# Weighing the values for two key blocks at a time in the second layer's attention, with sixteen places of exponentials

## The chip, the cores and the metric

The program runs on one core of a Trainium2 chip (NeuronCore 0 of one chip; the other cores are idle). The metric is the device time of one execution in microseconds, median of several runs. The program holds four layers; the change touches the attention of the second one (called layer 1 in the code, since counting starts at 0).

## The reference

Four layers, each `x = x + s * silu(ffn(xn))` with `s` an attention of the normalised input. The second layer's attention is a plain softmax attention over all keys (no causal mask), with 16 heads of 8 numbers each, 8 sequences of 512 tokens, after which only the 153 "most peaked" queries of a head keep their result:

```python
xn = _layernorm(x, axis=-1)
s = _L1_attn_ref(xn, Wq, bq, Wk, bk, Wv, bv, Wo, bo)    # scores, softmax, values; no mask
g = _silu(_L1_ffn_ref(xn, router_w, ...))                # routing to 64 small experts
x = x + s * g
```

For one head the part that matters here is: scores = q k^T (512 x 512), E = exp(scale * scores - maximum of the row), result = E^T v and the row sums of E, which come from a column of ones that is appended to v (hence 9 columns of values, 8 + 1).

## The kernel before, in words

`attend_phase` does this for both the first layer (causal) and the second (not causal, `maps = 1`). In the second layer the 128 pairs of sequence and head are worked on four at a time: 32 groups, called g below, of four heads each (UN = 4). The 512 tokens are four blocks of 128 (QT = 4). All engines run the same loop over groups, each in its own written order, and meet at semaphores.

For every group there are these steps:

- **First pass** (`pass1`, L686, TensorE): scores with queries in the rows, in 8 cells of two matrices 128 x 512 each, into `att_pS`, which has two places (SB = 2) for such a cell. VectorE takes the maximum of each row (`extreme`, L834, 128 x 1024 per cell) and frees the place. The first pass of group g + 2 is done while the exponentials of group g run.
- **Turning the maxima** (`turn_maxima`, L697, TensorE, waits for all 8 maxima of the group), and `negate` (L785, ScalarE); GpSimd then splits the maxima into three bf16 parts (L598, L601), and three DMAs (L569) put them beside the queries, as extra rows of the second product.
- **Second pass** (`pass2`, L708, TensorE): scores with keys in the rows, 16 cells c = 0..15 of 128 x 512 (cell c is key block c // 4 of head c % 4), into `att_pX`, which has three places (XB = 3). So `pass2` of cell c waits until the exponential of cell c - 3 is out of its place.
- **Exponentials** (`expo`, L779, ScalarE): one 128 x 512 instruction for each cell, from `att_pX` into `att_E`, which has NE places.
- **Weighing the values** (`weigh`, L721, TensorE): for one key block kt, four fp32 products of 9 x 512, one for each head, side by side in different columns of the array; each shows as two matmuls, so a call shows as x8. It waits until the exponentials of cells 4 kt to 4 kt + 3 are there. The four key blocks add up in `att_pO`.
- **Results**: ScalarE copies `att_pO` (`results`, L791, for the previous group), TensorE turns the copy (`turn_results`, L729), VectorE takes reciprocals and multiplies (`store`, L848, L851). Routing of the same layer's experts is done beside it on GpSimd and VectorE (L1546 to L1633).

The order of the work on TensorE is set by a loop over s = 0..15 for each group. In step s it first issues what PLAN[s] holds (a cell of the first pass at every even s; at s = 2 `turn_maxima` goes ahead of it, at s = 8 `turn_results`), then `pass2` of cell s + 1, and then whatever `WEIGHS` has under s. A key of 16 or more in `WEIGHS` means step s - 16 of the next group. On ScalarE, `expo` of cell s comes at step s, `negate` behind s = 1 and `results` behind s = RESULTS. Semaphores hold counts, so an engine can run ahead only as far as the places of `att_pX`, `att_pS` and `att_E` go.

Of the kernel before, what the change touches and what calls it, by code (L numbers as in the profile page):

```python
# [465 lines left out]
def attend_phase(nc, R, name, maps, arr, vtok, heads, lamb=None, negmax=None, aside=None):  # L466
# [13 lines left out]
    if causal:  # L480
        CELLS = [((0, 1, 2, 3), 0), ((0, 1), 1), ((0,), 2), ((2, 3), 1), ((1,), 2), ((0,), 3), ((2,), 2), ((3,), 2), ((1,), 3), ((2,), 3), ((3,), 3)]
        PLAN = ((0, 1),) + tuple((c,) for c in range(2, 11))
        XCELLS = [((x, 0),) for x in range(UN)] + [((x, 1), (x, 3)) for x in range(UN)] + [((x, 2), (x + 1, 2)) for x in range(0, UN, 2)]
        ORDER = (0, 1, 3, 2)
        WEIGHS = {7: (0,), 12: (1, 3, 2)}
        SEQ = (0, 1, "tops", 2, 3, 4, 5, 6, "turned", 7, 8, 9, 10)
        RESULTS, STORES = 3, {0: (0,), 1: (1,)}
        SB, XB = 4, 3
        NE = len(XCELLS)
    else:  # L490
        CELLS = [((x, x), j) for x in range(UN) for j in range(0, QT, 2)]
        PLAN = tuple((s // 2,) if s % 2 == 0 else () for s in range(16))
        XCELLS = [((x, kt),) for kt in range(QT) for x in range(UN)]
        ORDER = (0, 1, 2, 3)
        WEIGHS = {4: (0,), 8: (1,), 12: (2,), 16: (3,)}
        SEQ = (0, "tops", 1, 2, 3, "turned", 4, 5, 6, 7)
        RESULTS, STORES = 2, {0: (0, 1)}
        SB, XB = 2, 3
        NE = 8
    NP1, NP2 = len(CELLS), len(XCELLS)  # L500
    cell_of = {xk: c for c, cell in enumerate(XCELLS) for xk in cell}
    ready = {kt: 1 + max(c for (x, k), c in cell_of.items() if k == kt) for kt in range(QT)}
# [14 lines left out]
    with phase(nc, name) as p:  # L517
# [4 lines left out]
        mp = p.sb("mp", [IT, 2, 3, P], BF16)  # L522
        E = p.sb("E", [P, NE, T])
        vs = p.sb("vs", [P, 2, GH, QT, DV])
# [31 lines left out]
        with nc.Block() as block:  # L556
# [98 lines left out]
            def _(pe):  # L655
# [43 lines left out]
                def pass2(at, g, c, early):  # L699
                    k = (g * NP2 + c) % (NB * NP2)  # L700
                    bank, free = BANK2[k], g * NP2 + c + LAST2[k] + 1
                    if c == 0:
                        pe.wait_ge(s_mr[g % NB], at(48, 48 * (g // NB + 1)))
                    if not (early and free <= 0):
                        pe.wait_ge(s_e, at(NB * NP2, free))
                    for n, (x, kt) in enumerate(XCELLS[c]):
                        o, w = offset[x, kt], T - q0(kt)
                        ins = nc.tensor.matmul(pX[:, bank, o:o + w], ks[:, g % NB, x, kt * P:(kt + 1) * P], qs[:, g % NB, x, q0(kt):],  # L708
                                               start=(n == 0), stop=True, skip_group_check=True)
                    ins.then_inc(s_p2, 1)  # L710

                def weigh(at, g, kt, early):
                    if kt == 0:
                        pe.wait_ge(s_vs, of(at, 1, g, 1))
                        if not early:
                            pe.wait_ge(s_oT, of(at, 1, g, 0))
                    pe.wait_ge(s_cut if causal else s_e, of(at, NP2, g, ready[kt]))
                    w = T - q0(kt)
                    for x in range(UN):
                        o = offset[x, kt]  # L720
                        ins = nc.tensor.matmul(pO[32 * x:32 * x + DV, q0(kt):], vs[:, g % 2, x // maps, kt], E[:, cell_of[x, kt] % NE, o:o + w],  # L721
                                               start=(kt == ORDER[0]), stop=(kt == ORDER[-1]), tile_position=(0, 32 * x), skip_group_check=True)
                    ins.then_inc(s_pv, 1)
# [8 lines left out]
                def body(i, first, last):  # L732
# [9 lines left out]
                    for g in range(NB):  # L742
                        for s in range(NP2):
# [8 lines left out]
                            if not (last and h >= NB):  # L752
                                pass2(at, h, (s + 1) % NP2, first and h == 0)
                            for kt in WEIGHS.get(s + NP2, ()):
                                if not (first and g == 0):
                                    weigh(at, g - 1, kt, first and g == 1)
                            for kt in WEIGHS.get(s, ()):
                                weigh(at, g, kt, first and g == 0)
                    if last:
                        for s in range(NP2, 2 * NP2):  # L760
                            for kt in WEIGHS.get(s, ()):
                                weigh(at, NB - 1, kt, False)
# [5 lines left out]
            def _(act):  # L768
                def expo(at, g, c, first):
# [3 lines left out]
                    act.wait_ge(s_p2, of(at, NP2, g, c + 1))  # L773
                    if x == 0 and not (first and g == 0 and c < NE):
                        old = c - NE
                        held = max(ORDER.index(k) for _, k in XCELLS[old % NP2])
                        act.wait_ge(s_pv, of(at, QT, g, old // NP2 * QT + held + 1))
                    gain_of = x // maps
                    nc.scalar.activation(E[:, c % NE], pX[:, BANK2[(g * NP2 + c) % (NB * NP2)]], ACT.Exp, scale=gs[:, g % 2, gain_of:gain_of + 1]).then_inc(s_e, 1)  # L779

# [257 lines left out]
def layer0_attention(nc, R, t, early, out):  # L1038
    with ExitStack() as ctx:
        keep = lambda name, shape: ctx.enter_context(nc.sbuf_tensor(name, shape, F32))  # L1040
        heads = keep("heads0", [P, B * NH * QT, DH])
        vtok = keep("v0", [P, B * NH, QT, DH + 1])
        parts = nc.dram_tensor("parts0", (2, B * NH, 2, 3, DH, T), BF16).ap()
        with phase(nc, "arr0") as p:
            arr = Arrivals(p, 2, parts, R.ext0, t["gain0"], R.masks, t["later0"])
            project_phase(nc, R, "proj0", 4, early, parts, vtok, arr, qscale=True)
            attend_phase(nc, R, "att0", 2, arr, vtok, heads, lamb=R.lam)
        outproj_phase(nc, R, "out0", heads, out)
# [441 lines left out]
def layer1_attention(nc, R, t, early, out, sc, consts, s_in, comb, cT):  # L1490
    with ExitStack() as ctx:
        keep = lambda name, shape: ctx.enter_context(nc.sbuf_tensor(name, shape, F32))
        heads = keep("heads1", [P, B * NH * QT, DH])
        vtok = keep("v1", [P, B * NH, QT, DH + 1])
        negmax = keep("negmax", [P, B * NH * QT])
        total = keep("total", [P, B * QT, NH])
        mask = keep("mask1", [P, QT, B * NH])
        parts = nc.dram_tensor("parts1", (2, B * NH, 1, 3, DH, T), BF16).ap()
        with phase(nc, "arr1") as p:
            arr = Arrivals(p, 1, parts, R.ext1, t["gain1"])  # L1500
            project_phase(nc, R, "proj1", 2, early, parts, vtok, arr, mean={"sum": total})
            with routing(nc, "route", sc, consts, s_in, comb) as aside:
                attend_phase(nc, R, "att1", 1, arr, vtok, heads, negmax=negmax, aside=aside)
        with phase(nc, "spread") as p:
            pick_phase(nc, R, "pick", negmax, total, int(0.6 * 256), mask, comb, 64, cT, p.sem("out"))
        outproj_phase(nc, R, "out1", heads, out, mask=mask)
# [2170 lines left out]
```

## Time and profile before

| | us |
|---|---|
| median of 3 runs | 3879.37 (3876.12 to 3881.76) |
| the profiled execution | 3873.31 |
| its span, first to last instruction | 3871.5 |
| second layer's attention loop, first to last exponential | 1253.5 to 1674.5 |

In the span TensorE's matmuls are busy 87%, VectorE 61%, ScalarE 52%, GpSimd 40%. These shares are averages over stages with different limits; for this change only the stretch of the attention loop of the second layer matters. There `turn_maxima` (L697) comes once in every group, which makes it a good mark: it starts at 1272.22 us, and 29 groups later at 1653.2 us, which is 13.14 us for a group. Busy times of TensorE contain the drain of a matmul that overlaps the next one, so they are read for starts rather than for shares.

### The profile page before, as it was taken

Reading aid. Unit: us, or ns where it says so; the run is one execution under the profiler, and the core shown is the slowest. Engines: PE = TensorE matmul, PEld = TensorE weight load, DVE = VectorE, ACT = ScalarE, POOL = GpSimd, SP = SyncE. Lnnn points to the kernel's source line nnn. Section 1 sums busy time; section 2 is a strip of 40 time slices with the busy share of each in tenths; the row PEclk is TensorE's granted clock in tenths of the full one; section 3 lists DMA queues with packets and bytes.
Section 4 is the critical chain, followed back from the end, with each engine's and each line's share of the span. In section 5 each row is a group of like instructions: output and inputs, shape, how many; then the busy total and the mean of one; then the engine's idle time right before and its main releaser. Section 6 shows DMA issues by size and latency. Waiting matters only on the chain. (4 is left out here: it accounts for less than half of the span.)

```text
span 3871.5 us, 87522 instructions
## 1 busy us (share of the span) xinstructions
PE 3381.1 (87%) x26932; PEld 2090.2 (54%) x26932; DVE 2358.0 (61%) x5961; ACT 2030.5 (52%) x4194; POOL 1567.7 (40%) x2652
## 2 busy tenths in 40 slices
PE   5799999599966999959999947979874999999997
PEld 2344444477742222226777723579863666666664
DVE  5688887311135888856777765258356566666664
ACT  5588888333353788833333353333253566666552
POOL 0367676000010232316777717045472444444440
PEclk9799999799986999979999968877696999999999
DMA  5422222000013111116666411300023333333330
GB/s 138 102 73 74 73 73 54 12 6 12 6 36 89 45 44 46 41 27 173 163 156 161 117 58 37 102 12 3 9 50 55 127 115 114 118 115 113 114 101 22
DMA packets 199845, 289.31 MB, mean 75 GB/s; under 512 B 40954, under 2 KB 156864, under 8 KB 199252
## 3 DMA queue, kind: packets, MB, share of 16 engines
q1 hardware_dynamic: 195480, 277.41, 25.8%
q0 software_dynamic: 4096, 8.40, 1.5%
q8 instruction: 158, 2.59, 0.3%
q14 instruction: 111, 0.91, 0.1%
HBM read 234.41 MB, written 35.93 MB: 70 GB/s over the span
## 5 line engine op out<-in xcount | busy, mean ns | idle before, releaser
L779 ACT ACTIVATE att_E<-att_pX,att_gs 128x512 f32<-128x512 f32 x1152 | 718.7, 684 | 128.3 <-PE att_pX L708 127.6
L1958 POOL TENSOR_TENSOR att_E<-att_E,att_rz 128x128 f32<-128x128 f32 (+3 forms) x512 | 358.2, 721 | 433.6 <-DVE att_rz L2166 433.6
L834 DVE TENSOR_REDUCE att_mx<-att_pS 128x2 f32<-128x1024 f32 (+2 forms) x448 | 434.6, 991 | 82.2 <-PE att_pS L686 68.3
L686 PE MATMUL att_pS<-arr_ks,arr_qs 72*128 72x512 bf16 (+4 forms) x1536 | 421.4, 338 | 51.8 <-DVE att_mx L834 28.4
L708 PE MATMUL att_pX<-arr_qs,arr_ks 75*128 75x512 bf16 (+4 forms) x1536 | 419.2, 328 | 8.5 <-DMA arr_qs<-att_mp 4.4
L1698 POOL TENSOR_TENSOR pairs_h<-pairs_m,pairs_r 128x512 f32<-128x512 f32 x272 | 346.1, 1273 | 190.9 <-DVE pairs_m L1761 181.7
L1722 PEld LDWEIGHTS pairs_po<-pairs_a,pairs_h 128*128 128x128 f32 x2176 | 286.3, 192 | 130.3 <-issue 128.5
L826 DVE CUSTOM_DVE_ANT_0 att_seen<-att_pS,arr_later 128x384 bf16<-128x384 f32 (+1 forms) x512 | 298.8, 613 | 80.3 <-PE att_pS L686 79.9
L1743 ACT ACTIVATE pairs_r<-pairs_ph 128x512 f32<-128x512 f32 x272 | 162.6, 598 | 327.1 <-PE pairs_ph L1714 327.1
L721 PE MATMUL att_pO<-att_E,att_vs 128*9 128x512 f32 (+3 forms) x3072 | 296.8, 488 | 8.8 <-ACT att_E L779 8.4
L2097 ACT ACTIVATE att_E<-att_S,att_nm 128x128 f32<-128x128 f32 (+3 forms) x512 | 282.1, 556 | 39.6 <-DVE att_nm L2160 39.4
L1714 PE MATMUL pairs_ph<-xnT,pairs_a 128*128 128x512 f32 x544 | 281.4, 600 | 10.2 <-DMA pairs_a<-in_down_dram 10.2
L1722 PE MATMUL pairs_po<-pairs_a,pairs_h 128*128 128x128 f32 x2176 | 287.5, 275 | 0.3 <-POOL pairs_h L1698 0.3
L617 POOL TENSOR_SCALAR_AFFINE_SELECT att_E<-att_E 128x256 f32<-128x256 f32 (+1 forms) x640 | 228.5, 361 | 136.4 <-ACT att_E L779 131.1
L686 PEld LDWEIGHTS att_pS<-arr_ks,arr_qs 76*128 76x128 bf16 (+1 forms) x1536 | 133.9, 98 | 258.9 <-DVE att_mx L834 100.0
L1761 DVE SCALAR_TENSOR_TENSOR pairs_m<-pairs_ph,pairs_c 128x512 f32<-128x512 f32 x272 | 187.9, 692 | 140.4 <-ACT pairs_r L1743 132.2
L2160 DVE CUSTOM_DVE_ANT_0 att_S<-att_pS,att_bias 128x128 f32<-128x128 f32 (+3 forms) x512 | 230.5, 487 | 67.4 <-PE att_pS L2000 62.0
L708 PEld LDWEIGHTS att_pX<-arr_qs,arr_ks 127*128 127x128 bf16 (+1 forms) x1536 | 149.0, 98 | 217.0 <-ACT att_E L779 124.4
L1340 PEld LDWEIGHTS ex_po<-ex_a,ex_h 128*128 128x128 f32 x1536 | 201.6, 192 | 91.8 <-issue 91.0
L1366 ACT ACTIVATE ex_h<-ex_ph,ex_bs 128x512 f32<-128x512 f32 x192 | 132.0, 687 | 213.5 <-PE ex_ph L1331 213.5
L1382 DVE SCALAR_TENSOR_TENSOR f<-ex_po,ex_ws,f 128x128 f32<-128x128 f32 x192 | 54.1, 344 | 276.7 <-PE ex_po L1340 276.7
L2174 DVE COPY att_WT<-att_pT 128x128 f32<-128x128 f32 (+2 forms) x384 | 178.8, 507 | 66.2 <-PE att_pT L2010 59.0
(410 smaller groups left out, 6531.1 us busy)
## 6 DMA issues: line engine op xcount, KB each, us to landing
pairs_c<-weights SPq DMA_DIRECT2D x272, 256.0 KB, 4.0
att_bias<-in_bias_dram SPq DMA_DIRECT2D x64, 896.0 KB, 4.6
parts<-proj_part SPq DMA_DIRECT2D x144, 128.0 KB, 2.3
att_xb<-xnT SPq DMA_DIRECT2D x64, 256.0 KB, 2.7
arr_qs<-parts SPq DMA_DIRECT2D x192, 64.0 KB
arr_ks<-parts SPq DMA_DIRECT2D x192, 64.0 KB
att_w<-in_w3a_dram SPq DMA_DIRECT2D x64, 192.0 KB, 2.4
arr_qs<-parts SPq DMA_DIRECT2D x96, 96.0 KB
```

The lines of the kernel that those rows point to most:

```text
L686: ins = nc.tensor.matmul(pS[:, bank, n * w:(n + 1) * w], qs[:K1, u, x, q * P:(q + 1) * P], ks[:K1, u, x, :w], start=(n == 0 or not causal) ...
L708: ins = nc.tensor.matmul(pX[:, bank, o:o + w], ks[:, g % NB, x, kt * P:(kt + 1) * P], qs[:, g % NB, x, q0(kt):], start=(n == 0), stop=True ...
L721: ins = nc.tensor.matmul(pO[32 * x:32 * x + DV, q0(kt):], vs[:, g % 2, x // maps, kt], E[:, cell_of[x, kt] % NE, o:o + w], start=(kt == OR ...
L779: nc.scalar.activation(E[:, c % NE], pX[:, BANK2[(g * NP2 + c) % (NB * NP2)]], ACT.Exp, scale=gs[:, g % 2, gain_of:gain_of + 1]).then_inc( ...
L826: V.tensor_tensor_reduce(out=seen[:, own, :w], in0=pS[:, bank, :w], in1=arr.later[:, T - w:], scale=1.0, scalar=-3.0e38, op0=ALU.add, op1= ...
L834: V.reduce_max(dst, src, AX.X).then_inc(s_mx, 1)
L1698: nc.gpsimd.tensor_tensor(h[:, g % RING], m[:, g % RING], r[:, g % RING], ALU.mult).then_inc(s_h, 1)
L1714: nc.tensor.matmul(ph[:, g % RING], a[:, v, 0], R.xnT[:, b * T:(b + 1) * T], start=True, stop=True).then_inc(s_up, 1)
L1722: ins = nc.tensor.matmul(po[:, g % RING, q * P:(q + 1) * P], h[:, g % RING, q * P:(q + 1) * P], a[:, v, 1], start=True, stop=True)
L1958: nc.gpsimd.tensor_tensor(E[:, k, :width(j)], E[:, k, :width(j)], rz[:, u, k:k + 1].broadcast_to([P, width(j)]), ALU.mult).then_inc(s_n, 1)
L2097: nc.scalar.activation(E[:, k, :width(j)], S[:, r % RING, :width(j)], ACT.Exp, bias=nm[:, u, k:k + 1], scale=-1.0, accum_out=Z[:, u, k:k + ...
L2160: nc.vector.tensor_tensor_reduce(out=S[:, r % RING, :w_], in0=pS[:, r // 2 % 2, h, :w_], in1=bias[:, u, off:off + w_], scale=-1.0 / DW, sc ...
```

## The change

Four numbers in the branch for attention without a mask.

```diff
-        WEIGHS = {4: (0,), 8: (1,), 12: (2,), 16: (3,)}
+        WEIGHS = {9: (0, 1), 17: (2, 3)}
         SEQ = (0, "tops", 1, 2, 3, "turned", 4, 5, 6, 7)
-        RESULTS, STORES = 2, {0: (0, 1)}
+        RESULTS, STORES = 3, {0: (0, 1)}
         SB, XB = 2, 3
-        NE = 8
+        NE = 16
```

Key blocks 0 and 1 are weighed together at step 9, key blocks 2 and 3 together at step 1 of the next group. `att_E` gets 16 places instead of 8, since eight exponentials must now be kept until they are weighed. The copy of the results goes behind the exponential of cell 3 instead of cell 2. The instructions are the same in number and kind; the first layer's branch is not touched.

On TensorE, in the written-out first groups of the second layer's attention, around the step from one group to the next (`att_pX` is the second pass, `att_pS` the first pass, `att_pO` the weighing, `ident,att_mx` the turning of the maxima), there stood before:

```order
L721 MATMUL att_pO<-att_E,att_vs 9x512 x4
L708 MATMUL att_pX<-arr_qs,arr_ks 128x512
L686 MATMUL att_pS<-arr_ks,arr_qs 128x512 x2
L708 MATMUL att_pX<-arr_qs,arr_ks 128x512 x2
L686 MATMUL att_pS<-arr_ks,arr_qs 128x512 x2
L708 MATMUL att_pX<-arr_qs,arr_ks 128x512
L721 MATMUL att_pO<-att_E,att_vs 9x512 x4
L708 MATMUL att_pX<-arr_qs,arr_ks 128x512
L697 MATMUL att_pS<-ident,att_mx 16x128
L686 MATMUL att_pS<-arr_ks,arr_qs 128x512 x2
L708 MATMUL att_pX<-arr_qs,arr_ks 128x512 x2
```

And now at the same place:

```order
L721 MATMUL att_pO<-att_E,att_vs 9x512 x8
L686 MATMUL att_pS<-arr_ks,arr_qs 128x512 x2
L708 MATMUL att_pX<-arr_qs,arr_ks 128x512 x2
L686 MATMUL att_pS<-arr_ks,arr_qs 128x512 x2
L708 MATMUL att_pX<-arr_qs,arr_ks 128x512 x2
L686 MATMUL att_pS<-arr_ks,arr_qs 128x512 x2
L708 MATMUL att_pX<-arr_qs,arr_ks 128x512 x2
L686 MATMUL att_pS<-arr_ks,arr_qs 128x512 x2
L708 MATMUL att_pX<-arr_qs,arr_ks 128x512 x2
L721 MATMUL att_pO<-att_E,att_vs 9x512 x8
L697 MATMUL att_pS<-ident,att_mx 16x128
```

The weighing of two key blocks stands as one piece directly in front of the turning of the maxima, and a second-pass cell that stood between weighing and turning now stands ahead of the weighing. The other pair, the first row of the second piece, is followed by a first-pass cell and only then by second-pass cells; before, a second-pass cell always came first behind a weighing.

On ScalarE, in the same groups (`att_m<-att_pS` is `negate`, `att_oT<-att_pO` is `results`), before:

```order
L785 ACTIVATE att_m<-att_pS 16x128
L779 ACTIVATE att_E<-att_pX,att_gs 128x512
L791 ACTIVATE att_oT<-att_pO 128x512
L779 ACTIVATE att_E<-att_pX,att_gs 128x512 x15
L785 ACTIVATE att_m<-att_pS 16x128
```

And now:

```order
L785 ACTIVATE att_m<-att_pS 16x128
L779 ACTIVATE att_E<-att_pX,att_gs 128x512 x2
L791 ACTIVATE att_oT<-att_pO 128x512
L779 ACTIVATE att_E<-att_pX,att_gs 128x512 x14
L785 ACTIVATE att_m<-att_pS 16x128
```

Only the copy of the results has moved, by one exponential. VectorE, GpSimd and the DMA queue of SyncE have the same rows as before.

## Rows read from the trace of the kernel before

**Rows 1.** Stretches of the attention loop; busy us (instructions) by engine, clock, DMA

```profile
core 0: us, PE busy (x) PEld busy (x) DVE busy (x) ACT busy (x) POOL busy (x), PEclk, DMA share, GB/s
1256.00:1300.00 44.00, 40.66 (x210) 11.50 (x208) 34.28 (x59) 33.53 (x57) 10.88 (x31) 0.92 0.20 42
1300.00:1640.00 340.00, 317.35 (x1791) 95.60 (x1789) 285.23 (x458) 275.50 (x466) 102.65 (x293) 1.00 0.18 45
```

**Rows 2.** ScalarE's groups of instructions over 29 groups, 1272.2 to 1653.2

```profile
L779 ACT ACTIVATE att_E<-att_pX,att_gs 128x512 f32<-128x512 f32 x464 | 292.1, 681 | 57.9 <-PE att_pX L708 57.9
L791 ACT ACTIVATE att_oT<-att_pO 128x512 f32<-128x512 f32 x29 | 16.5, 570 | 0.0
L785 ACT ACTIVATE att_m<-att_pS 16x128 f32<-16x128 f32 x29 | 7.7, 267 | 14.5 <-PE att_pS L697 14.5
```

**Rows 3.** VectorE's and the weight loads' groups over the same 29 groups

```profile
L834 DVE TENSOR_REDUCE att_mx<-att_pS 128x2 f32<-128x1024 f32 x232 | 279.5, 1220 | 56.7 <-PE att_pS L686 55.0
L1613 DVE TENSOR_TENSOR route_eq<-route_gs 128x256 f32<-128x256 f32 x8 | 3.3, 412 | 0.0
...
L721 PEld LDWEIGHTS att_pO<-att_E,att_vs 128*9 128x9 f32 x928 | 14.0, 88 | 54.2 <-ACT att_E L779 37.0 <-issue 17.2
```

**Rows 4.** Timeline of one group, selected rows; idle before and releaser in brackets

```profile
1456.04 0.28 PE L697 MATMUL att_pS<-ident,att_mx 128*16 128x128 f32 x1
1456.35 0.27 ACT L785 ACTIVATE att_m<-att_pS 16x128 f32<-16x128 f32 x1 [0.43 <-PE att_pS L697]
1456.53 0.66 ACT L779 ACTIVATE att_E<-att_pX,att_gs 128x512 f32<-128x512 f32 x1
...
1457.10 0.57 ACT L791 ACTIVATE att_oT<-att_pO 128x512 f32<-128x512 f32 x1
1457.61 1.84 ACT L779 ACTIVATE att_E<-att_pX,att_gs 128x512 f32<-128x512 f32 x3
...
1458.37 1.05 PE L721 MATMUL att_pO<-att_E,att_vs 128*9 128x512 f32 x8
...
1459.04 1.78 SPq L569 DMA_DIRECT2D arr_qs<-att_mp  x3
...
1459.35 0.39 PE L708 MATMUL att_pX<-arr_qs,arr_ks 75*128 75x512 bf16 x1
...
1459.77 1.92 ACT L779 ACTIVATE att_E<-att_pX,att_gs 128x512 f32<-128x512 f32 x3 [0.32 <-PE att_pX L708]
...
1460.44 0.60 PE L729 MATMUL att_pS<-ident,att_oT 128*128 128x128 f32 x4
...
1461.49 0.60 PE L686 MATMUL att_pS<-arr_ks,arr_qs 72*128 72x512 bf16 x2 [0.45 <-DVE att_mx L834]
...
1462.35 0.69 ACT L779 ACTIVATE att_E<-att_pX,att_gs 128x512 f32<-128x512 f32 x1 [0.66 <-PE att_pX L708]
...
1463.65 2.50 ACT L779 ACTIVATE att_E<-att_pX,att_gs 128x512 f32<-128x512 f32 x4 [0.61 <-PE att_pX L708]
...
1464.08 2.36 DVE L834 TENSOR_REDUCE att_mx<-att_pS 128x2 f32<-128x1024 f32 x2 [0.72 <-PE att_pS L686]
...
1466.46 2.51 ACT L779 ACTIVATE att_E<-att_pX,att_gs 128x512 f32<-128x512 f32 x4 [0.32 <-PE att_pX L708]
...
1469.69 0.27 ACT L785 ACTIVATE att_m<-att_pS 16x128 f32<-16x128 f32 x1 [0.72 <-PE att_pS L697]
```

**Rows 5.** Timeline in the first layer: weighing of three key blocks in one piece

```profile
507.11 1.48 PE L721 MATMUL att_pO<-att_E,att_vs 128*9 128x384 f32 x24
508.53 0.34 PE L686 MATMUL att_pS<-arr_ks,arr_qs 76*128 76x384 bf16 x1
```

**Rows 6.** Timeline of the loop's first group and its end, and what follows the end

```profile
1260.02 1.90 PE L721 MATMUL att_pO<-att_E,att_vs 128*9 128x512 f32 x8
...
1675.23 1.04 PE L721 MATMUL att_pO<-att_E,att_vs 128*9 128x512 f32 x8 [1.14 <-ACT att_E L779]
1677.00 0.66 PE L729 MATMUL att_pS<-ident,att_oT 128*128 128x128 f32 x4 [0.72 <-ACT att_oT L791]
```

## The prediction

> **What bounds the kernel now.** I read the stretches of the attention loop first [rows 1]. From 1300 to 1640 us VectorE is busy 285.23 of 340 us (84%), ScalarE 275.50 (81%), GpSimd 102.65, and the granted clock is 1.00 throughout. No engine is full; TensorE's 317 us hold overlapped drains and say little. So the loop is held by engines that wait for each other, and what counts is who waits. The groups of ScalarE over 29 groups of heads [rows 2] say it: in 381.0 us, 13.14 a group, ScalarE sat idle 57.9 us for second-pass cells and 14.5 us for the turned maxima, together 2.50 us a group, and for nothing else. It never waited for a place in `att_E` or for `att_pO`. VectorE sat idle 55.0 us for first-pass cells [rows 3]. Both wait for TensorE, which works its list in order. The timeline of one group [rows 4] shows what stood in front each time. ScalarE's gaps are:
>
> - 0.43 (0.72 in the next group, 0.50 in the mean) ahead of `negate`: `turn_maxima` stands behind the weighing of block 3.
> - 0.32 ahead of exponential 6, and 0.32 ahead of 14: the second-pass cell stands behind the weighing of blocks 0 and 2.
> - 0.66 and 0.61 ahead of 9 and 10: TensorE turns the results, waits 0.45 for VectorE with first-pass cell 4, then weighs block 1.
>
> They sum to 2.34 with the 0.43, and to 2.63 with the 0.72 that the next group shows.
>
> **Durations**, all from rows 4. Exponentials follow each other by (2.50 - 0.69) / 3 = 0.60 us, `negate` takes 1456.53 - 1456.35 = 0.18 of ScalarE's line, `results` 0.51. A 128 x 512 bf16 product takes 0.60 - 0.39 = 0.21 of TensorE's line and is there 0.39 after its start; ScalarE starts 0.03 later. Weighing starts at 1458.37, and the next product at 1459.35: 0.98. A turned maximum is there after 0.28. Exponential 3 started at 1457.61 and frees ScalarE at 1458.21, and the weighing that needs it starts 0.16 later; I use 0.18 from "ScalarE could go on" to "TensorE may start". VectorE's maxima follow each other by 2.36 - 1.22 = 1.14 (1.22 is the mean of rows 3).
>
> These reproduce two gaps of before. Behind the weighing of block 0: 0.18 + 0.98 + 0.39 + 0.03 = 1.58, and ScalarE has two cells in hand (1.21): gap 0.37, the row says 0.32. Ahead of `negate`: 0.18 + 0.98 + 0.21 (a second-pass cell) + 0.31 = 1.68, less 1.21: 0.47, the rows say 0.43 to 0.72.
>
> **Weighing two blocks in one piece** is not in this loop, but the first layer weighs three blocks in one piece, 384 + 128 + 256 = 768 columns, in 508.53 - 507.11 = 1.42 us [rows 5]. Against 0.98 for 512 columns that is 0.44 / 256 = 1.72 ns a column, so 1024 columns take 0.98 + 0.88 = 1.86. The bounds are 1.96 (two single pieces) and 1.76 (1.72 ns each, no start at all). I take 1.86, as rows 5 are the same form. So TensorE saves 0.10 for each pair, 0.20 a group.
>
> **The change, part by part.** Sixteen places of `att_E`: worth nothing by themselves, since no wait for a place shows [rows 2]. Moving `results` by one exponential: nothing, it waits for nothing now and would still be late enough (below). What costs is the length of the piece against the three places of `att_pX`: when TensorE is away for 1.86 us, ScalarE has at most 3 x 0.60 = 1.81 in hand, and the second-pass cell isn't the first thing behind the piece any more.
>
> I walk a group from the moment 0 at which ScalarE is through with exponential 15.
>
> *Ahead of `negate`.* TensorE gets cell 15's place at 0.18, does second-pass cell 2 (to 0.39), weighs blocks 2 and 3 (to 2.25), turns the maxima; `negate` can start at 2.25 + 0.31 = 2.56. ScalarE ran out at 1.21. Gap 1.35, where it was 0.50.
>
> *Up to exponential 8.* `negate` 0.18, exponentials 2 and 3, `results` 0.51 (block 3 was weighed by 2.3, so no wait), exponentials 4 to 7: ScalarE is at 2.56 + 0.18 + 0.51 + 6 x 0.604 = 6.87. No weighing stands in steps 2 to 8, so the gaps ahead of 6, 9 and 10 are gone. VectorE gets first-pass cell 1 at 2.47 + 0.63 = 3.10 and does cells 1, 2, 3 by 6.52. First-pass cell 4 waits for the place of cell 3 as before, starts at about 6.64 and ends at 7.07; second-pass cells 9 and 10 follow, and cell 9 is just in time for ScalarE (7.49 against 7.47).
>
> *Ahead of exponential 11.* Weighing starts at 7.50, ends at 9.36; first-pass cell 5 takes 0.43; second-pass cell 11 is read at 9.79 + 0.42 = 10.21. ScalarE did 8, 9 and 10 by 8.68. Gap 1.53. If VectorE hadn't held TensorE up, it would be 0.18 + 0.21 + 1.86 + 0.43 + 0.42 - 1.81 = 1.29. Exponentials 11 to 15 then run through.
>
> So the gaps are 1.35 + 1.53 = 2.88 a group against 2.50. One group in four VectorE also has two routing comparisons of 0.41 [rows 3], which come just behind cell 4 in the order; I add 0.07 a group. My walk makes the gaps of before about 0.05 too long in one place of two (0.37 for 0.32), so I take off 0.05: +0.40 a group. The chain for the next group's maxima (GpSimd, then the DMAs issued at 1459.04) starts 0.85 later against ScalarE's line; its rows must be there for cell 0 of the next group some 9 us after the issue, and land long before [rows 4].
>
> *Sum.* 31 groups x 0.40 = 12.4 us. At the end of the loop, behind the last exponential, two blocks are weighed instead of one: +0.88. At its start the clock is at its lower level (1.2 GHz: 1.90 for a weighing instead of 1.05 [rows 6], mean clock 0.92 over 44 us [rows 1]), and a weighing of that time now comes after the rise: about -0.9. The two cancel. Profiled execution: 3873.3 + 12.4 = 3885.7 us. The median of the runs is 6.1 above the profiled execution, so I expect **3891.5 us** for it, +0.3%.
>
> **Bounds of this case.** With 1.76 for the pair and VectorE never late, 0.44 less a group: 0 us. With 1.96 and 0.2 more for routing: +0.8 a group, 25 us. So 3880 to 3904.
>
> **Rivals.**
>
> 1. *Faster: TensorE's order is the bound, and the joined piece takes waits out of it.* For it: weight loads of the weighing sat idle 37.0 us for an exponential [rows 3], 1.28 a group, four waits. In the new order the piece stands behind a second-pass cell that waits for the same exponential, so the piece has no wait of its own. If half of them go and the 0.20 is saved too, 0.84 x 31 = 26 us: 3853. Against it: TensorE waited there because it was ahead; ScalarE's gaps come from what follows. It decides if ScalarE's two new gaps stay under 1.2 each. Chance 0.12. The Trainium skill (Perfetto Trace Analysis, Matmul Optimizations) advises matmuls back to back in batches because of the clock, which speaks for this rival; the row shows a granted clock of 1.00 already, so by the rule there is nothing for the clock to give, and no number above rests on it.
> 2. *The same: VectorE decides.* It is busiest (84%), and with two first-pass cells in hand (2.28) it can ride over a piece of 1.86. If the round goes by VectorE, ScalarE's gaps only join into fewer and longer ones: 3879. Against it: VectorE's own idle time, 56.7 us for 29 groups, is waiting for TensorE, and my walk gives it a new wait of over 1 us behind the first piece. Chance 0.17.
> 3. *Slower by more: the clock.* At the lower level a weighing costs 0.85 more [rows 6]. If longer pauses of TensorE let the clock fall in one group of four, 8 groups with two pairs at +1.7 add 27 us: 3918. In the loop the clock never fell though waits of 0.4 to 0.9 us are all over it. Chance 0.03.
>
> The forecast itself has 0.68. A measurement of this kernel tells a change from none at about 0.2%, 8 us. Within the forecast's case about one in ten lies under that. Slower by over 0.2%: 0.63; within: 0.22 (rival 2 and the low end); faster: 0.15 (rival 1, and 0.03 for what I don't see). The range for 8 in 10: 3871 to 3902, which takes in rival 2 and leaves out rivals 1 and 3.
>
> **What would show it.** `turn_maxima` to `turn_maxima` 13.5 us instead of 13.14. ScalarE's idle ahead of L785 about 1.35 a group (14.5 us becomes about 39), ahead of L779 about 1.5 a group in one gap of three exponentials after the piece, and none ahead of 6 and 14. The piece 1.86 us from its start to the next product. No idle of ScalarE for `att_pO`. The granted clock 1.00. All other stages within a microsecond. I would be wrong if the gap ahead of exponential 11 is under 1 us, or if the gaps ahead of 9 and 10 stay beside it (then slower still), or if VectorE's idle time falls.

## The result and the profile after

The changed kernel takes 3904.86 us (median of 4 runs, 3899.36 to 3911.84), before 3879.3: ratio 1.0067, interval 1.0048 to 1.0087. Slower, as forecast, but by 25.6 us where 12.4 were forecast, and outside the range (3871 to 3902). The profiled execution took 3901.73 us with a span of 3900.0, 28.5 more than before's.

Where they lie is read from the same marks in both traces: the first exponential of the second layer, the `turn_maxima` that open and close 29 groups, the last exponential, and the first row of the last stage at 3857.3 and 3885.8 us.

| stretch | before, us | after, us | more |
|---|---|---|---|
| up to the first exponential | 1253.5 | 1260.0 | 6.5 |
| from there to `turn_maxima` of the third group | 18.74 | 19.63 | 0.89 |
| 29 groups | 381.02 | 398.45 | 17.43 |
| to the last exponential | 21.3 | 24.2 | 2.9 |
| the rest of the program | 2182.8 | 2183.5 | 0.7 |

The 6.5 us ahead of the loop are code that the change doesn't touch. In the 14 profiles below this mark lies between 1254.7 and 1260.5 us with no order by kernel (the changed kernel itself had 1260.0 here and 1254.7 when run again), so I don't count them to the change. The loop itself is 21.2 us longer.

`turn_maxima` to `turn_maxima` in the loop, in order (one pattern of four groups, since routing is spread over four):

```text
before     13.24 12.96 13.34 12.96 | repeated, mean 13.13, no exception behind the first groups
after      14.06 13.22 13.55 13.37 | repeated, mean 13.55,
           but once 17.24 and once 15.71 in the place of 14.06
```

In both rows the first number is the group in which VectorE does the two routing comparisons (L1612, L1613). A group of over 15 us is called long below, and a fall is a drop of the granted clock to its lower level.

This is the first of the two long groups:

```profile
1550.78 0.28 PE L697 MATMUL att_pS<-ident,att_mx 128*16 128x128 f32 x1
...
1553.93 0.52 DVE L1612 TENSOR_TENSOR route_gt<-route_gs 128x256 f32<-128x256 f32 x1
...
1554.37 0.41 DVE L1613 TENSOR_TENSOR route_eq<-route_gs 128x256 f32<-128x256 f32 x1
1554.39 0.60 PE L729 MATMUL att_pS<-ident,att_oT 128*128 128x128 f32 x4
1554.70 1.21 DVE L834 TENSOR_REDUCE att_mx<-att_pS 128x2 f32<-128x1024 f32 x1
...
1555.97 1.04 PE L686 MATMUL att_pS<-arr_ks,arr_qs 72*128 72x512 bf16 x2 [0.98 <-DVE att_mx L834]
...
1557.79 3.60 PE L721 MATMUL att_pO<-att_E,att_vs 128*9 128x512 f32 x16
...
1562.82 4.15 ACT L779 ACTIVATE att_E<-att_pX,att_gs 128x512 f32<-128x512 f32 x7 [4.08 <-PE att_pX L708]
1568.02 0.28 PE L697 MATMUL att_pS<-ident,att_mx 128*16 128x128 f32 x1
```

TensorE stands still for 0.98 us, for VectorE's maxima of first-pass cell 3, which come behind the two routing comparisons. From then on its products take longer (1.04 for a pair instead of 0.60), the joined weighing 3.60 instead of 1.91, and ScalarE waits 4.08 us. The stretches say the same; the last three columns are granted clock, DMA share and GB/s:

```profile
1550.00:1555.00 5.00, 4.63 (x25) 1.58 (x17) 4.28 (x9) 3.91 (x8) 2.05 (x7) 1.00 0.29 60
1555.00:1560.00 5.00, 4.03 (x16) 0.88 (x20) 2.60 (x4) 2.08 (x4) 0.00 (x0) 0.58 0.01 2
1560.00:1565.00 5.00, 4.89 (x21) 1.35 (x14) 2.60 (x3) 2.19 (x4) 0.00 (x0) 0.74 0.00 0
```

The comparisons stand at the same place in the kernel before, and TensorE waits for them there too, 0.73 us:

```profile
1433.56 0.41 DVE L1612 TENSOR_TENSOR route_gt<-route_gs 128x256 f32<-128x256 f32 x1
...
1433.89 0.41 DVE L1613 TENSOR_TENSOR route_eq<-route_gs 128x256 f32<-128x256 f32 x1
...
1434.22 1.21 DVE L834 TENSOR_REDUCE att_mx<-att_pS 128x2 f32<-128x1024 f32 x1
...
1435.49 0.61 PE L686 MATMUL att_pS<-arr_ks,arr_qs 72*128 72x512 bf16 x2 [0.73 <-DVE att_mx L834]
```

An undisturbed group of the changed kernel, without the comparisons, is the counterpart of [rows 4]:

```profile
1469.63 0.28 PE L697 MATMUL att_pS<-ident,att_mx 128*16 128x128 f32 x1
...
1469.94 0.27 ACT L785 ACTIVATE att_m<-att_pS 16x128 f32<-16x128 f32 x1 [1.41 <-PE att_pS L697]
...
1471.78 4.39 ACT L779 ACTIVATE att_E<-att_pX,att_gs 128x512 f32<-128x512 f32 x7
...
1475.02 1.91 PE L721 MATMUL att_pO<-att_E,att_vs 128*9 128x512 f32 x16
...
1476.86 0.60 PE L686 MATMUL att_pS<-arr_ks,arr_qs 72*128 72x512 bf16 x2
...
1477.50 2.36 DVE L834 TENSOR_REDUCE att_mx<-att_pS 128x2 f32<-128x1024 f32 x2 [1.58 <-PE att_pS L686]
1477.72 4.21 ACT L779 ACTIVATE att_E<-att_pX,att_gs 128x512 f32<-128x512 f32 x7 [1.54 <-PE att_pX L708]
```

Here the walk of the prediction can be read off: gap ahead of `negate` 1.41 (1.35 forecast), seven exponentials 4 to 10 in one run (the timeline joins them over a gap of 0.13 ahead of 9), the piece 1476.86 - 1475.02 = 1.84 (1.86), one gap of 1.54 ahead of exponential 11 (1.53), VectorE's new wait of 1.58. ScalarE over the 20 groups from 1279.6, to set against [rows 2]:

```profile
L779 ACT ACTIVATE att_E<-att_pX,att_gs 128x512 f32<-128x512 f32 x320 | 192.7, 682 | 37.6 <-PE att_pX L708 35.9
...
L785 ACT ACTIVATE att_m<-att_pS 16x128 f32<-16x128 f32 x20 | 5.3, 266 | 29.7 <-PE att_pS L697 29.7
```

### The profile page after: what moved, and what is told of

Same layout as the page of the kernel before. It is cut to its first block and busy times, and to the rows that moved or that the text cites. A ratio compares the mean times of both kernels' runs of the same rounds, so it can differ in the third digit from the quotient of the medians.

```text
span 3900.0 us, 87526 instructions
## 1 busy us (share of the span) xinstructions
PE 3398.1 (87%) x26932; PEld 2095.0 (54%) x26932; DVE 2353.3 (60%) x5961; ACT 2014.7 (52%) x4194; POOL 1564.3 (40%) x2652
## 5 line engine op out<-in xcount | busy, mean ns | idle before, releaser
L779 ACT ACTIVATE att_E<-att_pX,att_gs 128x512 f32<-128x512 f32 x1152 | 705.0, 684 | 135.2 <-PE att_pX L708 131.9
```

## The experiments

The ratio is the time over that of the kernel before on the same chip. "Group" is the mean of one undisturbed pattern of four groups in the profile. "Long groups" leaves out the first two groups and the last two.

| run | ratio (interval) | group, us | long groups |
|---|---|---|---|
| ne16 | 1.0000 (0.9991 to 1.0009) | 13.13 | none |
| late_singles | 0.9994 (0.9985 to 1.0003) | 13.17 | none |
| pair_first | 1.0070 (1.0056 to 1.0084) | 13.37 | 15.72 to 15.74 x4, 17.29, 17.22 |
| pair_second | 1.0043 (1.0029 to 1.0056) | 13.73 | none |
| pairs_again (the changed kernel) | 1.0082 (1.0068 to 1.0096) | 13.55 | 17.11, 15.70, 17.08, 15.71 |
| pairs_compare_late | 1.0041 (1.0027 to 1.0054) | 13.36 | none |
| pair_first_compare_late | 1.0015 (1.0006 to 1.0024) | 13.21 | none |
| spread | 0.9944 (0.9930 to 0.9957) | 12.62 | none |
| spread_neg1 | 0.9959 (0.9945 to 0.9973) | 12.73 | none |
| before_neg2 | 0.9996 (0.9987 to 1.0005) | 13.11 | none |
| spread_compare_late | 0.9938 (0.9924 to 0.9951) | 12.51 | none |
| pairs_neg2 | 1.0063 (1.0049 to 1.0077) | 13.56 | 17.27, 15.72 |
| before_compares_doubled | 1.0047 (1.0034 to 1.0061) | 13.29 | 15.48 x4 |
| pair_first_filled | 1.0065 (1.0052 to 1.0079) | 13.63 | none |

**Which part costs.** Edits to the kernel before:

```diff
 ne16:          NE = 16
 late_singles:  WEIGHS = {5: (0,), 9: (1,), 13: (2,), 17: (3,)}; RESULTS = 3; NE = 16
 pair_first:    WEIGHS = {9: (0, 1), 12: (2,), 16: (3,)}; NE = 16
 pair_second:   WEIGHS = {4: (0,), 8: (1,), 17: (2, 3)}; RESULTS = 3; NE = 16
```

> Kernel before with one number changed: 16 places for exponentials instead of 8. Theory A (what costs is the length of the joined weighing): ScalarE never waited for a place in att_E, so the time is that of before, ratio 1.000 (within 0.001), 13.14 us a group, and the first exponential of the second layer at about 1253.5 us. Theory B (the larger tile itself costs, by its place in memory or by setup, which would also explain that the changed kernel reached this loop 6.5 us later): ratio 1.002, first exponential at about 1260.

> Single weighings, but each as late as in the changed kernel or later: key blocks 0 to 3 at steps 5, 9, 13 and 17, results behind exponential 3, 16 places. Theory A (length of the piece): 13.1 us a group, ratio 1.000, ScalarE's idle ahead of the negation about 0.5 us. Theory C (what costs is that weighing and copy of the results come late): about 13.5 us a group, ratio 1.003 to 1.007.

> Only key blocks 0 and 1 are weighed together (step 9), blocks 2 and 3 stay at steps 12 and 16; results behind exponential 2 as before, 16 places. Theory A: half of the new waits, ahead of exponential 11 about 1.3 to 1.5 us, while those ahead of 9 and 10 go and the negation's stays at 0.5: 13.3 to 13.4 us a group, ratio 1.002. Theory D (the two pairs only cost through each other, since only two waits in a row starve VectorE): ratio 1.000.

> Only key blocks 2 and 3 are weighed together (step 17, in front of the turning of the maxima), blocks 0 and 1 stay at steps 4 and 8; results behind exponential 3, 16 places. Theory A: ScalarE's idle ahead of the negation 1.4 us as in the changed kernel, while the old gap ahead of 9 and 10 stays: 13.4 to 13.5 us a group, most of the whole loss, ratio 1.004. Theory D: 13.2 or less, ratio 1.000. Falls of the clock in the loop, if any, come in the group with the routing comparisons.

The 16 places cost nothing, nor do late single weighings and late results: theories B and C fall, theory A stands. Each pair alone costs more than half of the regular loss, so they don't add up (theory D falls): 13.37 and 13.73 alone, 13.55 together. That the second pair alone is dearer than both was not expected (13.4 to 13.5), and its cause stays open. The first pair alone was expected at 1.002 and came out at 1.0070, about as slow as both pairs, by its six long groups. Every one of them is a group with the comparisons.

**The clock.** Edit to the changed kernel and to pair_first:

```diff
-            elif k == 10:
+            elif k == 12:
                 dve.wait_ge(s_own, at(OWN, 6))      # the two comparisons L1612, L1613
```

> The changed kernel once more, to stand beside the next ones on the same chip. Ratio 1.0067 as before; regular groups 13.2 to 14.06 us in a pattern of four (13.55 in the mean), and every longer group (over 15 us) is one with the routing comparisons, one in four. How many of them are long may differ from run to run.

> The changed kernel with VectorE's two routing comparisons (0.41 us each) moved from behind first-pass cell 3 to behind cell 4, two odd steps later, where VectorE sits idle while TensorE weighs. Theory E (the clock falls where TensorE stands still for about 1 us waiting for VectorE's maxima of cell 3, just ahead of the first pair, and the pair then runs at the lower clock): no long group left behind the first two, the group of 14.06 comes down to about 13.5, the mean to about 13.4 us, ratio about 1.0035. Rival F (the clock falls at random or from the length of the pieces): long groups stay, ratio 1.006.

> Only key blocks 0 and 1 joined, as in the run pair_first with its seven or so long groups of 15.7 to 17.3 us, and the two routing comparisons moved two odd steps later. Theory E: no long groups, 13.2 us a group, ratio about 1.001 instead of 1.007. Rival F: long groups stay, ratio 1.006.

The text of pairs_compare_late names one place wrongly: by the trace the comparisons stood behind cell 2, in front of cell 3, and now stand behind cell 4, beside the piece. Both runs came out as theory E said, 1.0041 and 1.0015: no long group, and the group of 14.06 became 13.29. On one chip the ratio of the changed kernel falls from 1.0082 to 1.0041 by moving two VectorE instructions of 0.41 us that have nothing to do with the pairs.

But all kernels with long groups so far had two things together: eight steps without a weighing, and a standstill of over 0.9 us. (pair_second, with no weighing in steps 9 to 16 and no wait over 0.64 us in these groups, had none.) Two runs part them.

```diff
 before_compares_doubled:                    # kernel before; gx is a spare tile
+                for m in range(2):
+                    V.tensor_tensor(gx[:, m], each(gs[:, :, :]), other(gs[:, :, :]), ALU.is_gt)
 pair_first_filled:                          # pair_first
-                    for n, (x, kt) in enumerate(XCELLS[c]):
+                    for n, (x, kt) in list(enumerate(XCELLS[c])) * (5 if c == 8 and not causal else 1):
```

> Kernel before, with two more routing comparisons (0.41 us each, into a spare tile, results unused) in front of the two that are there, so that TensorE's wait for the maxima of cell 3 grows from 0.45 to about 1.2 us in one group of four, while a single weighing still stands between the turning of the maxima and that wait. Theory G (a wait of about 1 us alone makes the clock fall): some of these groups are long, over 15 us, ratio 1.003 or more. Theory H (the wait makes it fall only at the end of a stretch of eight steps without a weighing, as in the changed kernel): the group of 13.34 becomes about 14.1, none is over 15 us, the clock stays at 1.00 in the loop, ratio 1.0015.

> The run pair_first, with second-pass cell 8 computed five times over into its own place instead of once (0.85 us more of bf16 products just ahead of the wait for the maxima of cell 3; the values don't change). TensorE's wait of 1.15 us in the group with the comparisons is then about 0.3 us of waiting and 0.85 of work, and the group should end no later. If the standstill itself makes the clock fall, the long groups go: those groups 14.1 us, the others up to 0.6 longer than in pair_first (13.4 to 14.2), no group over 15. If the stretch without a weighing is enough, the long groups of 15.7 and 17.3 stay.

In these groups the standstill is what is needed: theory G holds, theory H falls. In the kernel before with the longer wait (its group with the comparisons was the one of 13.24, not of 13.34), TensorE stands still 1.39 us and the single weighing behind it takes 1.90 instead of 1.05:

```profile
1382.55 1.05 PE L721 MATMUL att_pO<-att_E,att_vs 128*9 128x512 f32 x8
...
1386.62 0.60 PE L686 MATMUL att_pS<-arr_ks,arr_qs 72*128 72x512 bf16 x2 [1.39 <-DVE att_mx L834]
...
1387.58 1.90 PE L721 MATMUL att_pO<-att_E,att_vs 128*9 128x512 f32 x8
```

Its stretches, with the granted clock before the last two columns:

```profile
1383.00:1387.00 4.00, 2.61 (x19) 1.12 (x12) 3.83 (x8) 2.56 (x5) 0.65 (x3) 1.00 0.15 25
1387.00:1391.00 4.00, 4.00 (x16) 0.75 (x14) 1.62 (x3) 1.38 (x2) 0.00 (x0) 0.57 0.00 0
```

In pair_first the same place, then the same place with the wait filled by repeated products; first pair_first:

```profile
1388.59 0.67 PE L686 MATMUL att_pS<-arr_ks,arr_qs 72*128 72x512 bf16 x2 [1.15 <-DVE att_mx L834]
...
1390.04 3.06 PE L721 MATMUL att_pO<-att_E,att_vs 128*9 128x512 f32 x16
```

And pair_first_filled:

```profile
1389.10 1.71 PE L708 MATMUL att_pX<-arr_qs,arr_ks 75*128 75x512 bf16 x6
...
1391.81 0.60 PE L686 MATMUL att_pS<-arr_ks,arr_qs 72*128 72x512 bf16 x2 [0.56 <-DVE att_mx L834]
...
1392.78 1.91 PE L721 MATMUL att_pO<-att_E,att_vs 128*9 128x512 f32 x16
```

That group took 14.09, as expected, and none was long. The ratio hardly fell (1.0065), since the filling costs 0.47 to 0.50 us in two of the other three groups and 0.10 in the third; the loop is as long as that of pair_first (443.4 and 443.2 us). For a kernel it is no cure.

What these runs leave open is whether it must be one standstill, or whether shorter waits close together do it too. The last two groups of the loop, where no first pass is left for TensorE to do, speak for the second. There the clock falls in every profile with a joined piece, with no wait of TensorE over 0.88 us. In pairs_compare_late it falls at 1670.6 us, behind waits of 0.49, 0.18 and 0.66 us:

```profile
1668.89 0.39 PE L708 MATMUL att_pX<-arr_qs,arr_ks 75*128 75x512 bf16 x1 [0.49 <-ACT att_E L779]
1669.46 0.39 PE L708 MATMUL att_pX<-arr_qs,arr_ks 75*128 75x512 bf16 x1 [0.18 <-ACT att_E L779]
1670.51 1.18 PE L708 MATMUL att_pX<-arr_qs,arr_ks 75*128 75x512 bf16 x2 [0.66 <-ACT att_E L779]
...
1673.33 3.60 PE L721 MATMUL att_pO<-att_E,att_vs 128*9 128x512 f32 x16
```

**Gaps by themselves, and a better order.** Edits to the kernel before:

```diff
 spread:       WEIGHS = {6: (0,), 10: (1,), 14: (2,), 17: (3,)}; NEGATE = 2
 spread_neg1:  the same WEIGHS, NEGATE = 1 as before
 before_neg2:  NEGATE = 2
 spread_compare_late:  spread, and k == 12 for k == 10
 pairs_neg2:   the changed kernel, NEGATE = 2
```

> Single weighings again, at steps 6, 10, 14 and 17, eight places, the negation behind exponential 2 instead of 1, results behind exponential 2. By the walk of the prediction with the same durations: behind every weighing ScalarE has more in hand, the turning of results no longer meets a weighing in the same stretch, and the negation doesn't wait behind a weighing: 12.3 to 12.5 us a group, 31 x 0.8 = 20 to 27 us less than before, ratio 0.993 to 0.995. Rival (VectorE, at 84 percent busy, is the true bound): 13.0 or more a group, ratio 0.999 to 1.0. Joined pieces are no part of it.

> The run spread with the negation back behind exponential 1: weighing at steps 6, 10, 14, 17, eight places. If the gain of spread (12.62 us a group) comes from the places of the weighings, this keeps most of it: 12.9 us a group, ratio 0.997, ScalarE's idle ahead of the negation about 0.6 us. If it comes from the negation, the ratio is 1.000.

> Kernel before with the negation behind exponential 2 instead of 1, nothing else. By the account of gaps alone 0.5 us a group would go (ratio 0.996). By the walk around the whole loop the gap ahead of the negation only moves to the next second-pass cell, since TensorE hands cells out no earlier: 13.1 us a group, ratio 0.999 to 1.000.

> The run spread and the two routing comparisons moved two odd steps later: both findings together. 0.1 us a group less than spread, 12.5 us, ratio about 0.9936, no group over 13 us behind the first two. If VectorE isn't late ahead of cell 4 any more in this order, nothing is gained: 0.9944.

> The changed kernel with the negation behind exponential 2 instead of 1. If each gap of ScalarE were a cost by itself (the prediction's account), 0.6 us of the 1.4 ahead of the negation would go in each group: regular groups 12.95 us, ratio 1.003. By the walk around the loop TensorE is late for its second-pass cells behind the piece anyway and waits for VectorE: regular groups 13.5 us, ratio 1.006 to 1.008, the long groups stay.

In before_neg2 the negation, moved behind one more exponential, takes away ScalarE's whole idle time ahead of it, and that time comes back ahead of the second-pass cells, 71.5 us for 57.9 [rows 2]:

```profile
L779 ACT ACTIVATE att_E<-att_pX,att_gs 128x512 f32<-128x512 f32 x464 | 292.9, 683 | 71.5 <-PE att_pX L708 71.3
...
L785 ACT ACTIVATE att_m<-att_pS 16x128 f32<-16x128 f32 x29 | 7.2, 249 | 0.0
```

In the changed kernel it is the same (13.56 for 13.55). So a gap of ScalarE isn't a price by itself; that TensorE and VectorE set when the cells come is how I read it. Where the weighings stand does decide: at 6, 10, 14 and 17 with the negation left where it was (spread_neg1) the groups take 12.73 us (12.9 expected), with the negation moved too 12.62 (12.3 to 12.5 expected), and VectorE's idle for first-pass cells falls from 55.0 [rows 3] to 31.6 us over 29 groups:

```profile
L834 DVE TENSOR_REDUCE att_mx<-att_pS 128x2 f32<-128x1024 f32 x231 | 275.7, 1217 | 32.1 <-PE att_pS L686 31.6
```

spread and spread_compare_late beat both kernels, by 0.56% and 0.62%. They can't be told from each other by the time, only by the groups (12.62 and 12.51).

## Why the prediction was right and wrong

- **Direction and the walk of a group without comparisons: right.** The joined piece (1.84 us) and the two gaps are there in the size given (1.48 in the mean ahead of `negate`, 1.54 ahead of exponential 11), and the gaps ahead of 6, 10 and 14 are gone. ScalarE's two new gaps are not under 1.2 each, so rival 1 fell. VectorE did not carry the round: the changed kernel is slower by 0.42 a group, and spread runs it 0.5 us faster than before (rival 2 fell).
- **The regular term: the right number by luck.** Forecast +0.40 a group, measured 13.55 - 13.13 = +0.42. But ScalarE's idle time went from 2.50 to (37.6 + 29.7) / 20 = 3.37, +0.87, and not +0.38. Of the surplus 0.34 is a gap ahead of exponential 9 that the walk had as gone (1.01 in the group with the comparisons, about 0.12 in the others), and 0.13 is ahead of `negate`. Against it stands busy time that fell by 0.45 a group: two gaps fewer (3 for 5), and exponentials of one run that follow each other at 0.575 us instead of 0.600; why they do is open. The sum of gaps left out both. (The forecast of 3891.5 is 0.3 under its own sum, 3873.3 + 12.4 + 6.1.)
- **The comparisons and the clock: the step that failed.** The prediction says that the two routing comparisons "come just behind cell 4 in the order" and adds 0.07 a group. They stand behind cell 2, in front of cell 3, and so in front of the very wait for which the walk holds TensorE up ahead of cell 4. In the kernel before this wait was already 0.73 in their group, where rows 4, a group without them, show 0.45. In the changed kernel it is 0.98, and the clock, which the sum has at nothing (rival 3, chance 0.03), fell behind it. The mechanism that rival 3 names is what came: "longer pauses of TensorE let the clock fall in one group of four". That "waits of 0.4 to 0.9 us are all over it" was no guard against it: TensorE's longest wait in the 29 groups was 0.73. Size: 17.24 - 14.06 and 15.71 - 14.06 are 4.8 us of the profiled execution, and four long groups make 9.4 us in pairs_again. As time alone the comparisons cost 0.13 a group more than before (0.69 / 4 less 0.15 / 4) where 0.07 was forecast. pairs_compare_late puts them where the prediction had them: 13.36 a group, no long group, ratio 1.0041, which is 16.0 us and within the range.
- **Start and end: forecast 0, measured 0.9 + 2.9 = 3.8 us,** of which 0.8 is the regular term of two groups. In pairs_again it is 2.3 + 4.0, in pairs_compare_late 3.0 + 5.7, more than its 6.3 in the 29 groups; so there too the total is near the forecast for other reasons than the forecast had. "A weighing of that time now comes after the rise" was wrong: the first piece starts at 1270.55 and the clock rises at 1272.51, 12.5 us behind the first exponential (rows below), where it took 9.8 before. That the late weighing holds the rise back is not shown: pair_second weighs its first block 7.1 us behind the first exponential, before 6.5, and its clock rises only after 15.4. The +0.88 of the end was to come behind the last exponential; the 2.9 lie ahead of it, where the clock falls twice and didn't before. The 0.7 in the rest of the program may hold the 0.88; no run parts it.

```profile
1266.00:1270.00 4.00, 3.53 (x10) 0.96 (x8) 2.39 (x3) 2.53 (x4) 0.43 (x3) 0.50 0.02 3
1270.00:1274.00 4.00, 4.00 (x22) 0.77 (x21) 1.46 (x4) 1.26 (x2) 0.00 (x0) 0.69 0.01 2
1274.00:1278.00 4.00, 3.57 (x18) 1.12 (x20) 4.00 (x9) 3.81 (x7) 0.00 (x0) 1.00 0.15 52
```

Of the 17.4 us in the 29 groups 29 x 0.42 = 12.2 are regular, 4.8 are the falls, and 0.4 are left. The loop's 21.2 us stand against 25.6 between the medians; the difference lies within the spread of the runs, and with four falls, in pairs_again, the loop is 28.1 us longer than the one before.

## What to carry to other kernels

When engines wait on each other in a ring, don't add up the gaps of one engine: walk one round with all of them, and check the walk by moving one instruction that should change nothing (before_neg2). Walk the worst group too, with the rare work (the comparisons here) at the place where the trace has it: one group in four decided this case. When a change removes work in front of a wait of TensorE, work out how long that wait becomes there, since here a standstill of about a microsecond cost 1.6 to 3.2 us at the lower clock. Work that only fills another engine's time belongs where that engine waits anyway.

## What the runs showed of the hardware

The granted clock fell from 2.4 to 1.2 GHz in the middle of a loop that keeps TensorE busy around it, after single standstills of 0.97 to 1.39 us. In the full groups it never fell after shorter ones: 0.56 us, 0.73 (five times in the kernel before), 0.81 (six times in before_neg2). It didn't fall after each long one either: of the eight groups with the comparisons it fell in two in the changed kernel's profile and in four when run again, in two in pairs_neg2, in six in pair_first, in four in before_compares_doubled. The last weighing of the kernel before, behind a wait of 1.14 us [rows 6], took 1.04, as at the higher clock. Near the loop's end, with less work for TensorE, shorter waits close together were enough (0.49, 0.18 and 0.66 us in pairs_compare_late). A fall cost 1.6 us or 3.0 to 3.2 us where a joined weighing followed, and 1.57 (15.48 - 13.91) where a single one did. At the loop's start the clock rose between 8.8 and 16.2 us behind the first exponential in the 16 profiles; what decides it is open.
